# Moving four transposes behind a projection in TensorE's step of a gated recurrent block

## The chip, the cores and the metric

The kernel runs on one core of a Trainium2 chip. The time is device microseconds of one execution. The kernel before was run three times: 1324.55, 1326.75 and 1327.91 us. The engines of the core work side by side and wait for each other by semaphores: TensorE (PE), VectorE (DVE), ScalarE (ACT), GpSimd (POOL) and SyncE (SP), which issues DMAs. GpSimd issues DMAs as well.

## The reference, cut to what matters

One block over a sequence of 2048 tokens of width 512: a layer norm, an attention-like part with 16 heads of 128 over four lags, a feed-forward part with weights reduced to their signs, and their product added to the input.

```
xn = layernorm(x)                                  # 2048 x 512
q, k, v = silu(xn @ Wq), silu(xn @ Wk), silu(xn @ Wv)   # 2048 x (16*128)
z, a, b = xn @ Wz, xn @ Wa, xn @ Wb
q, k, v = causal conv of 4 taps, per channel
q, k = rotary embedding of each
q = q / max(norm(q), 1e-12); k = k / max(norm(k), 1e-12)   # per head
for s in range(4):                                 # lags
    out += (sum(q * lag(k, s)) * scale * sigmoid(lag(a, s) * b)) * lag(v, s)
out = out * rsqrt(mean(out**2) + 1e-6) * norm_w * silu(z)
s = out @ Wout
g = silu((relu((xn @ sign(up).T) * up_scale) @ sign(down).T) * down_scale * output_scale)
y = x + s * g
```

## The kernel before, in words

The attention part runs in 64 steps, 16 heads (h) times 4 chunks of 512 tokens (g); c = 4h + g is the number of the step. Every engine has its own program of 64 steps, written by hand, and each engine carries out its program strictly in the order in which it is written (`schedule`, L349). The work on one block (a head and a chunk) is spread over four steps: `back(h, g, k)` gives the block of k steps ago, named at1, at2 and at3.

PE's step (L1070) was: project q, k and v of this block, each of them 12 matmuls of 512 columns (three products of high and low parts over four tiles of the width); `turn_fold` of block c-1; project z of block c-2; `score` of block c-2; `sum_values` of block c-3. Block c-2's z takes the PSUM bank that k has just left, so PE waits for the silu of k.

The folded squares belong to the norms of q and k. ScalarE squares the rotated halves of q and k into two arrays (L703, L704), a DMA of GpSimd adds one to the other (L568), and `turn_fold` (L1047) turns the sum with four transposes of 128 columns, so that tokens lie on partitions. DVE's `sum_fold` (L839) reduces what PE has turned to norms; GpSimd makes reciprocal roots of them (L528, L532), which pass through DRAM by DMAs of SyncE and come back as part of the gates (L548 to L556) a step later.

`score` (L1057) makes a band of scores between k and q, four fp32 matmuls of 132 columns. All blocks use the same PSUM buffer for them. So PE's score of block c-2 waits until DVE has read the scores of block c-3 (`gated`, L1063). DVE reads them in `gate_scores` (L854) and masks the result in `mask_band` (L864), which `sum_values` (L1034) waits for.

DVE's step (L880) has this order: tap 1 of q; v turned; rotation of k, with taps 2 and 3 of q between; tap 1 of k; `sum_fold` of block c-1; tap 2 of k; `gate_scores` and `mask_band` of block c-3; tap 3 of k; at g = 3 the low part of the next head's weights of q; taps of v and rotation of q; `join_out` and `make_o` of block c-3; more low parts of weights.

The two lines of this that tie the engines:

```
        def sum_fold(g1, c):
            wait(dve, turned_f, c)          # PE: turn_fold of this step
        ...
        def score(g2, k):                   # in step c, k = c - 2
            wait(pe, gated, k)              # DVE: gate_scores of block c - 3, this step
```

After the 64 steps PE, DVE and the others finish the last blocks in an order of their own (L1107 to L1124), and then come the feed-forward part and the output projection.

Of the kernel before, what the change touches and what calls it, by code (L numbers as in the profile page):

```python
# [205 lines left out]
def attention(nc, env):  # L206
# [135 lines left out]
    def back(h, g, k):  # L342

        h2, g2 = (h, g - k) if g >= k else (h - 1, g - k + G)
        if isinstance(h2, int) and not 0 <= h2 < H:
            return None
        return h2, g2
# [11 lines left out]
    def is_start(h, g):  # L359
        return isinstance(h, int) and h == 0 and g == 0  # L360
# [7 lines left out]
    def cols(g):  # L368
        return slice(g * CH, (g + 1) * CH)
# [599 lines left out]
    def on_tensor(pe):  # L969
# [22 lines left out]
        def project(n, bank, h, g, c, terms=range(TERMS)):  # L992
            if terms[0] == 0:
                wait(pe, wlo_done[n], h + 1)
            for i in terms:
                w, part = ((w_hi, x_hi), (w_lo, x_hi), (w_hi, x_lo))[i // KT]
                last = nc.tensor.matmul(bank[:, :], w[n][:, i % KT, :], part[:, i % KT, cols(g)],  # L997
                                        start=(i == 0), stop=(i == TERMS - 1))
            if terms[-1] == TERMS - 1:
                last.then_inc(proj_done[n], 1)  # L1000
# [33 lines left out]
        def sum_values(g3, c):  # L1034

            wait(pe, coef_done, c - 2)
            wait_v(pe, g3, c - 3)
            wait(pe, o_done, c - 3)
            wait(pe, out_sq_done, c - 3)
            for b in range(BC):  # L1040
                at = b % 2 * P
                last = nc.tensor.matmul(two[:, b // 2, at:at + BW], v_tok[:, g3 * BC + b, :],  # L1042
                                        coef[:, g3 % 2, b, :], start=(b % 2 == 0),
                                        stop=(b % 2 == 1), skip_group_check=True)
            last.then_inc(out_done, 1)

        def turn_fold(g1, c):  # L1047
            wait(pe, norms_done, c - 1)
            if isinstance(c, int) and c == NC:
                pe.wait_ge(folded_last, 1)  # L1050
            else:
                wait(pe, folded, 16 * c)
            for b in range(BC):
                last = nc.tensor.transpose(bank_tk[:, b * P:(b + 1) * P], fold[g1 % 2][:, b * P:(b + 1) * P], ident)  # L1054
            last.then_inc(turned_f, 1)

        def score(g2, k):  # L1057
            ahead = 1 if g2 < G - 1 else 0
            wait_rope(pe, "k", g2, k)
            wait_rope(pe, "q", g2, k)  # L1060
            if ahead:
                wait_rope(pe, "q", g2 + 1, k + 1)
            wait(pe, gated, k)  # L1063
            for b in range(BC):
                at = (g2 * BC + b) * P
                last = nc.tensor.matmul(scores[:, b, :], rot["k"][:, at:at + P], rot["q"][:, at:at + BW],  # L1066
                                        start=True, stop=True)
            last.then_inc(scores_done, 1)

        def step(h, g):  # L1070
            c = h * G + g
            at1, at2, at3 = (back(h, g, k) for k in (1, 2, 3))
            if not is_start(h, g):
                wait(pe, silu_done["v"], 2 * c)
                project("q", bank_qv, h, g, c)
            if is_start(h, g - 1):
                pe.wait_ge(bx_done, LAGS + 1)
                for i in range(2):
                    own = bx[:, i * HALF_NB:(i + 1) * HALF_NB, :, :].rearrange("p b h r -> p (b h r)")
                    after = bx[:, i * HALF_NB + 1:(i + 1) * HALF_NB + 1, :, :].rearrange(  # L1080
                        "p b h r -> p (b h r)")
                    nc.tensor.matmul(pick_banks[i], sel_own, own, start=True, stop=False)
                    nc.tensor.matmul(pick_banks[i], sel_next, after, start=False, stop=True
                                     ).then_inc(picked, 1)
            if not is_start(h, g):
                wait(pe, z_done, c - 2)
                project("k", bank_kz, h, g, c)
            wait(pe, silu_done["q"], 2 * c + 2)
            project("v", bank_qv, h, g, c)
            if is_start(h, g):  # L1090
                pe.wait_ge(abt_done, G)
                for b in range(NB):
                    last = nc.tensor.transpose(bank_ab[:, b * AB:(b + 1) * AB], ab_t[:, b * P:(b + 1) * P],
                                               ident[0:AB, 0:AB])
                last.then_inc(ab_turned, 1)
            if at1:
                turn_fold(at1[1], c)
            if at2:
                wait(pe, silu_done["k"], 2 * c + 2)
                project("z", bank_kz, at2[0], at2[1], c - 2)  # L1100
            if at2:
                score(at2[1], c - 2)
            if at3:
                sum_values(at3[1], c)

        schedule(pe, step)
        wait(pe, z_done, NC - 2)  # L1107
        project("z", bank_kz, H - 1, G - 2, NC - 2)
# [497 lines left out]
```

## Time and profile before

| | |
|---|---|
| median of 3 runs | 1326.75 us |
| the profiled execution | 1327.47 us |
| its span, first to last instruction | 1325.7 us |
| mean granted clock of PE | 0.995 |
| busy: PE, DVE, ACT, POOL | 1292.8, 954.7, 720.5, 641.8 us |

A matmul's record starts when the engine takes it up and its end is modelled, so records of neighbouring matmuls overlap. Distances between starts are the safer measure. The granted clock is a share of full speed: 1.00 is 2.4 GHz and 0.50 is 1.2 GHz. The number after `x` in a timeline row is how many instructions it merges; square brackets give the idle time of the engine before the row and what ended it.

### The profile page before, as it was taken

To read this page: it belongs to the slowest core of one execution; us is meant where nothing else is said; L and a number is where in the kernel's file an instruction comes from. 1 tells how busy PE (TensorE), PEld (TensorE's weight loads), DVE (VectorE), ACT (ScalarE), POOL (GpSimd) and SP (SyncE) were. 2 spreads that over 40 slices of the span, in tenths; PEclk is the share of its full clock that TensorE was granted. 3 is DMA by queue.
4 is the path that set the end of the run, shared out by engine and by line. 5 is a ranking of instruction groups with operands and counts; after the bars stand their busy time and mean duration, and the time that the engine had idled before them with its cause. 6 is when DMAs were issued, how large, how long until landed. Compare 5 with 4: busy or idle time off the path is not lost.

```text
span 1325.7 us, 22085 instructions
## 1 busy us (share of the span) xinstructions
PE 1292.8 (98%) x6312; PEld 1078.7 (81%) x6312; DVE 954.7 (72%) x1530; ACT 720.5 (54%) x1377; POOL 641.8 (48%) x827
## 2 busy tenths in 40 slices
PE   6989999999999999999999999998999999999998
PEld 5778888888888888888888888877888888888886
DVE  7879999989999999899999998993122322423442
ACT  5656666666666666666666666664543444422221
POOL 6357676777776767767767777763000000000001
PEclk9989999999999999999999999999999999999999
DMA  8258888888797888787878787868510101246544
GB/s 267 63 108 174 157 157 157 169 149 171 139 177 149 163 155 166 153 170 142 174 153 162 150 164 154 153 121 221 178 47 18 47 16 56 85 154 213 184 124 138
DMA packets 276875, 188.89 MB, mean 142 GB/s; under 512 B 167904, under 2 KB 204768, under 8 KB 276576
## 3 DMA queue, kind: packets, MB, share of 16 engines
q1 hardware_dynamic: 238064, 121.48, 34.1%
q0 software_dynamic: 38768, 66.87, 31.1%
q8 instruction: 23, 0.38, 0.1%
q14 instruction: 20, 0.16, 0.1%
HBM read 79.36 MB, written 42.08 MB: 92 GB/s over the span
## 4 chain that ended last, share of the span: by engine, by line
PE 77%; DVE 11%; issue 5%; DMA 3%; POOL 2%; ACT 2%; SPq 1%; DVEq 0%; POOLq 0%; ACTq 0%
PE bank L997 37%; PE bank L1491 13%; PE bank L1294 9%; PE bank L1281 8%; PE bank L1066 3%; PE bank L1042 3%; DVE y_k L812 2%; DVE y_q L812 2%; PE bank L1054 2%; DVE y_v L812 2%; PE bank L987 1%; ACT y_q L676 1%; DMA rq_win<-rq_scratch 1%; DVE coef L858 1%; DVE rot_k L831 1%
## 5 line engine op out<-in xcount | busy, mean ns | idle before, releaser
L812 DVE SCALAR_TENSOR_TENSOR y_q<-u_q,cw_q,y_q 128x512 f32<-128x512 f32 x192 | 143.0, 745 | 57.7 <-ACT y_q L676 57.6
L1362 POOL TENSOR_TENSOR g_buf<-g_buf,up_raw 128x512 f32<-128x512 f32 x3 | 3.8, 1280 | 356.2 <-DVE g_buf L1422 356.2
L1270 DVE TENSOR_TENSOR hid_lo<-relu,hid_hi 128x512 fp32r<-128x512 f32 x64 | 44.3, 693 | 166.4 <-ACT hid_hi L1262 166.4
L812 DVE SCALAR_TENSOR_TENSOR y_k<-u_k,cw_k,y_k 128x512 f32<-128x512 f32 x192 | 143.4, 747 | 1.3 <-ACT y_k L676 1.1
L812 DVE SCALAR_TENSOR_TENSOR y_v<-u_v,cw_v,y_v 128x512 f32<-128x512 f32 x192 | 143.4, 747 | 0.6
L532 POOL TENSOR_TENSOR rnorm<-norms,neg_half 128x8 f32<-128x8 f32 x64 | 125.0, 1953 | 9.6 <-POOL norms L528 8.6
L574 POOL DMA_DIRECT2D rot_q<-swapped_q x128 | 107.5, 996 | 43.4 <-DVE swapped_q L835 24.1
L574 POOL DMA_DIRECT2D rot_k<-swapped_k x128 | 107.3, 977 | 38.9 <-issue 25.3
L1258 ACT ACTIVATE relu<-bank,us_sb 128x512 f32<-128x512 f32 x64 | 44.1, 690 | 126.3 <-PE bank L1281 119.2
L568 POOL DMA_DIRECT2D down_raw<-down_raw x63 | 59.2, 940 | 91.0 <-ACT down_raw L704 81.4
L1382 ACT ACTIVATE hid_hi<-o_raw 128x512 fp32r<-128x512 f32 x64 | 40.2, 630 | 115.9 <-PE bank L1491 95.2
L1442 DVE TENSOR_TENSOR hid_lo<-o_raw,hid_hi 128x512 fp32r<-128x512 f32 x64 | 43.8, 690 | 79.9 <-ACT hid_hi L1382 79.9
L1491 PE MATMUL bank<-x_hi,hid_hi 128*128 128x512 f32 x256 | 99.6, 389 | 0.0
L1491 PE MATMUL bank<-x_hi,hid_lo 128*128 128x512 f32 x256 | 99.6, 389 | 0.0
L1491 PE MATMUL bank<-x_lo,hid_hi 128*128 128x512 f32 x256 | 99.6, 389 | 0.0
L528 POOL TENSOR_SCALAR norms<-norms 128x8 f32<-128x8 f32 x64 | 97.2, 1518 | 4.9 <-DVE norms L842 4.9
L562 POOL DMA_DIRECT2D sq_sum<-out_sq x62 | 90.9, 1467 | 2.5 <-issue 2.5
L662 ACT ACTIVATE u_v<-bank 128x512 f32<-128x512 f32 x64 | 38.4, 600 | 71.0 <-PE bank L997 71.0
L1066 PEld LDWEIGHTS bank<-rot_q,rot_k 128*128 128x128 f32 x512 | 68.1, 191 | 10.3 <-issue 5.5
L997 PE MATMUL bank<-x_hi,whi_z 128*128 128x512 f32 x256 | 75.6, 417 | 0.0
L1294 PE MATMUL bank<-down_sign_b,hid_hi 128*128 128x512 f32 x192 | 74.8, 390 | 0.4 <-DVE hid_lo L1270 0.4
L1294 PE MATMUL bank<-down_sign_b,hid_lo 128*128 128x512 f32 x192 | 74.7, 389 | 0.0
(189 smaller groups left out, 3514.8 us busy)
## 6 DMA issues: line engine op xcount, KB each, us to landing
rot_q<-swapped_q POOLq DMA_DIRECT2D x128, 128.0 KB, 4.5
v_scratch<-y_v SPq DMA_DIRECT2D x64, 256.0 KB, 3.6
rot_k<-swapped_k POOLq DMA_DIRECT2D x128, 128.0 KB, 4.1
v_tok<-v_scratch SPq DMA_DIRECT2D x256, 64.0 KB, 3.8
o_scratch<-o_buf SPq DMA_DIRECT2D x64, 256.0 KB, 3.5
o_raw<-o_scratch SPq DMA_DIRECT2D x64, 256.0 KB, 4.2
down_raw<-down_raw POOLq DMA_DIRECT2D x63, 256.0 KB, 3.4
sq_sum<-out_sq POOLq DMA_DIRECT2D x62, 256.0 KB, 5.4
```

The source lines that it names most:

```text
L528: nc.gpsimd.tensor_scalar(norms[:, g1 % 2, :], norms[:, g1 % 2, :], NORM_FLOOR, None, ALU.max).then_inc(floor_done, 1)
L532: nc.gpsimd.tensor_tensor(rnorm[:, g1 % 2, :], norms[:, g1 % 2, :], neg_half[:, 0:2 * BC], ALU.pow).then_inc(root_done, 1)
L562: nc.gpsimd.dma_start(sq_sum[:, cols(g)], squares, accum_op=ALU.add).then_inc(sq_added, 16)
L568: nc.gpsimd.dma_start(fold[g1 % 2], other[g1 % 2], accum_op=ALU.add).then_inc(folded, 16)
L574: nc.gpsimd.dma_start(rot[n][to:to + HALF, cols(g1)], swapped[n][frm:frm + HALF, g1 % 2, :], accum_op=ALU.add).then_inc(rope_added[n][g1 % ...
L812: nc.vector.scalar_tensor_tensor(y[n][:, g % 2, :], u[n][:, g % 2, i:i + CH], cw[n][:, bass.ds(h * TAPS + i, 1)], y[n][:, g % 2, :], ALU.m ...
L997: last = nc.tensor.matmul(bank[:, :], w[n][:, i % KT, :], part[:, i % KT, cols(g)], start=(i == 0), stop=(i == TERMS - 1))
L1066: last = nc.tensor.matmul(scores[:, b, :], rot["k"][:, at:at + P], rot["q"][:, at:at + BW], start=True, stop=True)
L1270: nc.vector.tensor_tensor(hid_lo[:, j % HS, :], relu[:, j % 2, :], hid_hi[:, j % HS, :].bitcast(fp32), ALU.subtract).then_inc(hid_lo_done, 1)
L1281: last = nc.tensor.matmul(up_bank(n, j), up_group(j // WG)[:, t, j % WG * P:(j % WG + 1) * P], part[:, t, bass.ds(n * CH, CH)], start=(k = ...
L1294: last = nc.tensor.matmul(acc_of(n)[b], part[:, j % HS, b * P:(b + 1) * P], down_group(j // WG)[:, j % WG, :], start=(j == 0 and part is h ...
L1491: last = nc.tensor.matmul(sums[b], part[:, h % HS, b * P:(b + 1) * P], wo_tile(w, h // KT, h % KT), start=(h == 0 and k == 0), stop=(h == ...
```

## The change

In PE's step the call of `turn_fold` moves from before the projection of z to behind it. Its waits (for the fold's DMA and for DVE's earlier reduction) move with it, and the wait for the silu of k now comes first. No other engine's program is touched.

```diff
@@ -1093,11 +1093,11 @@
                     last = nc.tensor.transpose(bank_ab[:, b * AB:(b + 1) * AB], ab_t[:, b * P:(b + 1) * P],
                                                ident[0:AB, 0:AB])
                 last.then_inc(ab_turned, 1)
-            if at1:
-                turn_fold(at1[1], c)
             if at2:
                 wait(pe, silu_done["k"], 2 * c + 2)
                 project("z", bank_kz, at2[0], at2[1], c - 2)
+            if at1:
+                turn_fold(at1[1], c)
             if at2:
                 score(at2[1], c - 2)
             if at3:
```

## Rows read from the trace of the kernel before

**Rows 1.** The page, the chain that ended last, by engine.

```profile
PE 77%; DVE 11%; issue 5%; DMA 3%; POOL 2%; ACT 2%; SPq 1%; DVEq 0%; POOLq 0%; ACTq 0%
```

**Rows 2.** Busy time by stretches: stretch, its length, each engine, clock, DMA share, GB/s.

```profile
350.00:450.00 100.00, 99.48 (x514) 83.97 (x513) 94.19 (x153) 64.31 (x129) 72.39 (x92) 1.00 0.83 163
```

**Rows 3.** Timeline of PE (start, length, line, what, count, idle before), one step.

```profile
403.01 1.07 PE L997 MATMUL bank<-x_hi,whi_v 128*128 128x512 f32 x4
...
405.73 0.60 PE L1054 MATMUL bank<-const,down_raw 128*128 128x128 f32 x4
406.09 1.17 PE L997 MATMUL bank<-x_hi,whi_z 128*128 128x512 f32 x4
...
408.92 1.07 PE L1066 MATMUL bank<-rot_q,rot_k 128*128 128x132 f32 x8
409.82 1.06 PE L1042 MATMUL bank<-coef,v_tok 128*128 128x132 f32 x8
410.64 1.17 PE L997 MATMUL bank<-x_hi,whi_q 128*128 128x512 f32 x4
...
413.89 1.17 PE L997 MATMUL bank<-x_hi,whi_k 128*128 128x512 f32 x4 [0.26 <-DVE wlo_k L823]
```

**Rows 4.** Timeline of all engines, DVE's and POOL's work between the transposes and scores.

```profile
406.46 0.68 DVE L842 TENSOR_REDUCE norms<-bank 128x8 f32<-128x512 f32 x1
...
407.06 0.74 DVE L812 SCALAR_TENSOR_TENSOR y_k<-u_k,cw_k,y_k 128x512 f32<-128x512 f32 x1
...
407.71 0.70 DVE L858 TENSOR_TENSOR coef<-bank,gates 128x528 f32<-128x528 f32 x1
...
413.06 0.68 DVE L823 TENSOR_TENSOR wlo_k<-raw_k,whi_k 128x512 fp32r<-128x512 f32 x1
...
418.48 0.38 POOL L556 TENSOR_TENSOR gates<-rq_own,gate_k 128x16 f32<-128x16 f32 x1 [0.25 <-POOL rq_own L551]
...
428.82 0.75 DVE L812 SCALAR_TENSOR_TENSOR y_q<-u_q,cw_q,y_q 128x512 f32<-128x512 f32 x1 [1.23 <-ACT y_q L676]
```

**Rows 5.** Timeline of PE and DVE in steps 1 and 2.

```profile
57.25 0.60 PE L1054 MATMUL bank<-const,down_raw 128*128 128x128 f32 x4
57.88 0.69 DVE L842 TENSOR_REDUCE norms<-bank 128x8 f32<-128x512 f32 x1 [0.90 <-PE bank L1054]
...
71.32 1.08 PE L1054 MATMUL bank<-const,down_raw 128*128 128x128 f32 x4 [4.18 <-DMA down_raw<-down_raw]
...
76.99 1.07 PE L1066 MATMUL bank<-rot_q,rot_k 128*128 128x132 f32 x8
```

**Rows 6.** Timeline of PE and DVE behind the last step.

```profile
894.66 0.63 PE L1054 MATMUL bank<-const,down_raw 128*128 128x128 f32 x4 [1.19 <-DVE down_raw L934]
...
901.81 0.71 DVE L858 TENSOR_TENSOR coef<-bank,gates 128x528 f32<-128x528 f32 x1 [4.90 <-POOL gates L556]
...
902.67 2.10 PE L1066 MATMUL bank<-rot_q,rot_k 128*128 128x132 f32 x8 [2.79 <-DVE coef L858]
...
906.09 1.17 PE L1281 MATMUL bank<-x_hi,up_sign_a 128*128 128x512 f32 x4
...
911.10 1.14 PE L1066 MATMUL bank<-rot_q,rot_k 128*128 128x132 f32 x8 [1.13 <-DVE coef L858]
...
912.90 1.18 PE L1281 MATMUL bank<-x_hi,up_sign_a 128*128 128x512 f32 x4
```

**Rows 7.** Timeline of PE ahead of the first step.

```profile
38.78 1.16 PE L987 MATMUL bank<-x_hi,whi_z 128*128 128x512 f32 x4 [1.46 <-issue]
```

**Rows 8.** Busy time by stretches of half a microsecond around two long pauses of PE.

```profile
69.50:70.00 0.50, 0.00 (x0) 0.00 (x0) 0.15 (x1) 0.49 (x2) 0.50 (x2) 0.73 1.05 258
...
73.50:74.00 0.50, 0.50 (x3) 0.40 (x2) 0.47 (x2) 0.00 (x0) 0.42 (x2) 0.50 0.00 0
...
902.50:903.00 0.50, 0.33 (x1) 0.36 (x2) 0.47 (x2) 0.50 (x1) 0.42 (x1) 0.59 1.02 327
...
906.00:906.50 0.50, 0.50 (x5) 0.46 (x4) 0.00 (x0) 0.13 (x1) 0.00 (x0) 1.00 0.48 77
```

## The prediction

> **What bounds the kernel now.** I read the chain of waits first, by engine: TensorE (PE) holds 77% of it [rows 1]. The busy time by stretches comes next: in the attention stage, from 150 to 850 us, seven stretches of 100 us all look alike, with PE busy for over 99 us, VectorE (DVE) for 93 to 94, and the granted clock at 1.00, which is 2.4 GHz [rows 2]. So PE is the bound and DVE is close behind it, with under 7% of slack. That small slack makes the order in which the two engines feed each other the thing to read, and for that I used the timeline of one step.
>
> PE's step, by starts [rows 3]: the projection of v takes 405.73 - 403.01 = 2.72 us, the four transposes 0.36, z 408.92 - 406.09 = 2.83, the scores 0.90, the sums over values 0.82, q 2.83 (it too follows short matmuls). With k at 2.72, a step is 2.72 x 2 + 2.83 x 2 + 0.36 + 0.90 + 0.82 = 13.18 us. Once per head k waits for its low weights: 413.89 - 410.64 - 2.83 = 0.42 us.
>
> DVE's order in the same step [rows 4]: sum_fold (L842), which reads the transposes, then the second tap of k, then the multiply of scores by gates (L858), then the mask. The scores have one buffer: score(c-2) waits in the code for `gated`, the multiply of this same step. So the chain is transposes -> L842 -> tap -> L858 -> scores. At present the projection of z, 2.83 us, stands between its two PE ends and hides it. L858 starts at 407.71 and the scores at 408.92, with nothing late.
>
> **What the change takes away.** z now follows v, both long, so z falls from 2.83 to v's 2.72: 0.11 us, in 61 steps (c = 3 to 63) 6.7 us [rows 3]. The wait for the silu of k moves ahead of the transposes with z; that silu runs while PE is still in v, so I cost it at nothing. silu_z gets its bank 0.36 us earlier, which nobody waits for.
>
> **What it adds: a wait.** The transposes now end PE's long work, and only they let L842 start. The links are each measured. From the transposes' start to L842 where DVE was waiting for them: 57.88 - 57.25 = 0.63 us [rows 5]. L842 to the tap 407.06 - 406.46 = 0.60, tap to L858 0.65 [rows 4]. L858 to the scores where PE was waiting for it: 902.67 - 901.81 = 0.86 [rows 6]. Sum 2.74 us, of which PE fills 0.36 with issuing the transposes. PE stands still for 2.38 us between issues; in the trace's own terms, the records end 0.60 after the transposes' start, so the shown pause would be about 2.14. After a pause, scores and values take 912.90 - 911.10 = 1.80 us against 410.64 - 408.92 = 1.72 [rows 3, 6]: 0.08 more. The mask follows L858 and is over before the values want it, as in that row.
>
> Steps that pay are those with an L858 in them and a turn_fold: c = 3 to 63, 61 of them. Net 2.38 - 0.11 + 0.08 = 2.35 us, x 61 = 143.4 us. The bounds of the stall are 0 (if L858 weren't behind L842 in DVE's order, which the code excludes) and 2.74 (if the transposes' issue hid nothing).
>
> Does the lateness grow on the other queues? DVE: everything behind L842 is late with it. In a normal step DVE now waits 1.23 us for q's tap (428.82) [rows 4]; the step grows by 2.35 us and DVE's work by nothing, so it stands at L842 ahead of the transposes and isn't a second bound. GpSimd: floor and power hang on L842's norms, SyncE's exchange of 1/|q| hangs on them, and the gates end 418.86 - 406.46 = 12.4 us after the reduction of the step before [rows 4]. The multiply that wants them comes a period plus 1.25 us after that reduction, at least 15.5 + 1.25. They are in time. The swapped halves and the folded squares start from work behind L858 or from q's taps and get more time before the scores and transposes that want them.
>
> The weights once per head: k's low half starts 413.06 - 407.71 = 5.35 us after L858 and k's projection 6.18 after it [rows 3, 4]. PE reaches k 0.86 + 1.80 + 2.83 = 5.49 after L858, so k would wait 0.69 rather than 0.42: 15 x 0.27 = 4.1 us. If scores and values run slower (below) PE arrives later than 6.18 and even the old 15 x 0.42 = 6.3 us go.
>
> **The start.** In step 2 PE idles 4.18 us until a fold's DMA lands, and only then does z, at half clock; scores start at 76.99 [rows 5]. With the change z runs in that pause. The next limit is the swapped q, whose DMAs are over at 73.5, as the DMA share falls to 0.00 there [rows 8]. So 76.99 - 73.5 = 3.5 us are gained once. Bounds: 0, and 5.3 (scores 0.36 behind the transposes of 71.32).
>
> **The clock.** Two long pauses of PE in this trace cost it its clock: after 4.18 us (0.73 in the half microsecond from 69.50) and after 2.79 us (0.59 from 902.50, back at 1.00 from 906.00) [rows 5, 6, 8]. Pauses of 1.13, 1.19 and 1.46 us did not [rows 6, 7]. The new one, 2.14 in the same terms, lies midway. But the 2.79 us had full-length matmuls on its front side, and the new pause has short ones on both sides, transposes ahead and 1.80 us of scores and values behind, so PE does less around it. And it comes back every step. I take it that the clock is lost in most steps. The price of one loss: scores and values took 906.09 - 902.67 = 3.42 us at 1.2 GHz against 1.80 at 2.4, so 1.62 us [rows 6]. Bounds over the stage: 0 and 61 x 1.62 = 98.8. I take 56 of 61 losses, 90.7 us.
>
> The Trainium skill, "TensorE: Matmul & The Clock Gate", section "Why this matters for your kernels", warns only of idle gaps longer than the one worked out here. By that rule the clock stays at 2.4 GHz and rival A below is the outcome. The trace has no pause of this size to decide it; its 2.79 us is shorter than the page's limit and did lose the clock, so I lean against the rule.
>
> **Sum**, against the profiled execution (1327.47 us, its span 1325.7): 1327.5 + 143.4 (wait, net) - 3.5 (start) + 90.7 (clock) - 6.3 (k's wait covered) = 1551.8. The profiled execution is 0.7 above the median, so against the median I say 1551.
>
> **The rivals.**
> A. The clock holds. Same wait, no loss: 1327.5 + 143.4 - 3.5 + 4.1 = 1471.5, about 1471. For it: 1.46 us was harmless. Against: 2.79 wasn't.
> B. The clock falls in some steps only, a third to two thirds: 20 to 40 losses, 32 to 65 us, with k's wait partly kept: 1500 to 1535. It would need the same pause to lose the clock at one time and keep it at another.
> C. Faster: the short matmuls stand together at no wait. One mechanism: PE reaches the scores no earlier than L858 + 0.86, because L842 is off DVE's road to L858. Then only the 0.11 us x 61 and the start count: 1327.5 - 6.7 - 3.5 = 1317. It decides where transposes to L858 take less than the transposes themselves, 0.36 us; the links measured sum to 1.88 to L858's start. Only a misreading of DVE's order would bring it.
> D. The change does not do what it says: short matmuls together save nothing, since scores and values need the same time behind transposes as behind z. That moves the sum by under 7 us and isn't told apart by the time.
>
> **How the numbers follow.** Forecast (clock lost nearly everywhere, 1535 to 1565) 0.60; B 0.17; A 0.18; C 0.02; beyond 1570, by something late that I've not seen, 0.03. The range must reach A to hold 8 in 10 with some room: 1466 to 1568. The likeliest case's own range is 1535 to 1565. About 0.3% (4 us) is what can be told from no change here. Faster 0.02, same 0.01, slower 0.97.
>
> **What would show it.** Order on PE: v, z, then L1054, L1066, L1042. Before L1066 a pause of some 2.1 us released by L858, in 61 steps. Before L842 on DVE a wait for L1054 in each. z's twelve matmuls 2.72 us. A step of 15.5 us where the clock is 1.00 and some 17.1 where it fell. PE's busy share down to some 86% of a step, and the granted clock below 1.00 in the attention slices, near 0.9. What follows the last scores unchanged, 1325.7 - 911.1 = 415 us. The prediction is wrong if L1066 isn't released by L858, if the pause is under 1.5 us, or if the clock stays at 1.00 throughout (then A).

## The result: 1551.2 us, and the profile after

The changed kernel takes 1551.16 us (1550.53 to 1554.31, 4 runs) against 1327.33 us for the kernel before on the same chip. The ratio is 1.1691, 95% interval 1.1675 to 1.1707: 17% slower.

The page of the changed kernel, in four rows: the busy time of the engines, the granted clock in 40 slices, the chain that ended last by engine, and the costliest group with the idle time ahead of it.

```profile
PE 1390.5 (90%) x6312; PEld 1165.4 (75%) x6312; DVE 962.0 (62%) x1530; ACT 717.9 (46%) x1377; POOL 612.7 (40%) x827
PEclk9999899989998998899999989988999999999999
PE 87%; DVE 7%; issue 4%; DMA 1%; POOL 1%; ACT 0%; SPq 0%; DVEq 0%; POOLq 0%
L1066 PE MATMUL bank<-rot_q,rot_k 128*128 128x132 f32 x512 | 99.2, 353 | 137.3 <-DVE coef L858 136.6
```

The scores (L1066) did not head any list before. Now PE idles 136.6 us for L858 just ahead of them. In the second row each digit is one of 40 slices, and a 9 stands for 90% or more; the eight digits of 8, all within the attention stage, are slices whose mean clock was under 0.9. That PE's share of the chain rose from 77% [rows 1] to 87% is no sign of more work: it is the same 6312 matmuls, some of them at half clock.

One stretch of 700 us inside that stage, first of the kernel before and then of the changed one (busy time of PE's matmuls, its weight loads, DVE, ACT and POOL, then clock, DMA share and GB/s, as in [rows 2]):

```profile
150.00:850.00 700.00, 696.72 (x3580) 588.32 (x3579) 653.00 (x1053) 444.57 (x893) 505.05 (x634) 1.00 0.83 159
```

```profile
150.00:850.00 700.00, 610.48 (x2792) 517.75 (x2791) 514.70 (x823) 346.36 (x699) 375.27 (x492) 0.91 0.63 124
```

PE is busy 87% instead of 99.5%, at a clock of 0.91. DVE falls from 93% to 74%, so it did not become the bound.

PE's timeline over one step of the changed kernel, to be laid beside [rows 3]:

```profile
474.70 1.07 PE L997 MATMUL bank<-x_lo,whi_v 128*128 128x512 f32 x4
475.61 1.07 PE L997 MATMUL bank<-x_hi,whi_z 128*128 128x512 f32 x4
...
478.33 0.60 PE L1054 MATMUL bank<-const,down_raw 128*128 128x128 f32 x4
481.08 1.96 PE L1066 MATMUL bank<-rot_q,rot_k 128*128 128x132 f32 x8 [2.15 <-DVE coef L858]
482.83 1.96 PE L1042 MATMUL bank<-coef,v_tok 128*128 128x132 f32 x8
484.44 1.27 PE L997 MATMUL bank<-x_hi,whi_q 128*128 128x512 f32 x4
...
495.55 0.60 PE L1054 MATMUL bank<-const,down_raw 128*128 128x128 f32 x4
```

z takes 478.33 - 475.61 = 2.72 us. Scores stand 2.75 us behind the transposes, with a recorded pause of 2.15. The two short groups take 484.44 - 481.08 = 3.36 us where they took 1.72. The step is 495.55 - 478.33 = 17.22 us long.

DVE and GpSimd in the same step, with the chain that makes the pause [rows 4]:

```profile
478.96 0.69 DVE L842 TENSOR_REDUCE norms<-bank 128x8 f32<-128x512 f32 x1 [2.59 <-PE bank L1054]
479.57 0.74 DVE L812 SCALAR_TENSOR_TENSOR y_k<-u_k,cw_k,y_k 128x512 f32<-128x512 f32 x1
...
480.23 0.70 DVE L858 TENSOR_TENSOR coef<-bank,gates 128x528 f32<-128x528 f32 x1
...
490.28 0.23 POOL L556 TENSOR_TENSOR gates<-rq_own,gate_k 128x16 f32<-128x16 f32 x1
```

The links are 0.63, 0.61, 0.66 and 0.85 us. The 2.59 us in brackets is DVE standing at the reduction; the tap and the multiply behind it then start with no wait of their own, so what they need was ready. The order of one engine's work, not its load, sets the end.

The clock around the same pause (half microseconds of the changed kernel):

```profile
480.50:481.00 0.50, 0.00 (x0) 0.00 (x0) 0.47 (x2) 0.00 (x0) 0.42 (x1) 1.00 0.01 0
481.00:481.50 0.50, 0.42 (x2) 0.45 (x3) 0.50 (x1) 0.00 (x0) 0.50 (x1) 0.73 0.00 0
481.50:482.00 0.50, 0.50 (x4) 0.50 (x4) 0.50 (x2) 0.00 (x0) 0.50 (x1) 0.50 0.00 0
...
484.50:485.00 0.50, 0.50 (x4) 0.46 (x3) 0.00 (x0) 0.18 (x1) 0.00 (x0) 0.86 0.00 0
485.00:485.50 0.50, 0.50 (x4) 0.41 (x3) 0.47 (x2) 0.48 (x2) 0.00 (x0) 1.00 0.00 0
```

PE is at 2.4 GHz while it stands still and falls to 1.2 GHz just as it has resumed. The half speed lies from about 481.23 to 484.64, 3.41 us, here on top of work. The mean granted clock of the whole span is 0.937, so (1 - 0.937) / 0.5 x 1549.1 = 195 us ran at 1.2 GHz, as much as 57 stretches of this length. The clock's own record in the trace has 56 of them, one in 56 of the 61 steps from 3 to 63, and a last one that reaches into the end of the span.

So five steps kept the clock, and their pause was no shorter. One of them, and the next to last scores of the stage, with the clock of three stretches:

```profile
532.67 1.14 PE L1066 MATMUL bank<-rot_q,rot_k 128*128 128x132 f32 x8 [2.15 <-DVE coef L858]
...
1127.48 1.14 PE L1066 MATMUL bank<-rot_q,rot_k 128*128 128x132 f32 x8 [2.81 <-DVE coef L858]
```

```profile
532.00:548.00 16.00, 13.41 (x68) 11.23 (x68) 13.01 (x21) 8.45 (x17) 9.74 (x14) 1.00 0.66 129
548.00:565.00 17.00, 15.01 (x68) 12.59 (x68) 11.70 (x20) 8.85 (x18) 9.00 (x13) 0.90 0.62 112
1126.00:1131.00 5.00, 3.52 (x24) 3.27 (x25) 1.66 (x3) 1.38 (x3) 1.36 (x3) 1.00 1.02 206
```

A step without the loss takes 548.23 - 532.67 = 15.56 us from scores to scores, and one with it 17.20 (the median, outside the steps that wait for k's weights): one loss costs 1.64 us. The pause of 2.81 us, behind long matmuls, did not cost the clock, where the one of 2.79 at the same place of the kernel before did [rows 6, 8]. Over the ten profiles of this case the pause at this place is 2.79 to 2.83 us; seven lost the clock around it and three kept it (this kernel and, below, the reduction between mask and tap 3 and the late reduction with PE's old order). The length of the pause alone does not decide. In the trace the half speed also begins at another place of each step: 1.27 us behind the start of the scores at 548.23, then a little earlier from step to step, until it begins 0.19 ahead of them at 720.35; the step after that one keeps the clock. What sets this place was not tested.

The 223.4 us between the two spans (1549.1 and 1325.7) are divided below, from scores to scores. Rows of the changed kernel, step 2 and the end, beside [rows 5, 6]:

```profile
57.77 0.60 PE L1054 MATMUL bank<-const,down_raw 128*128 128x128 f32 x4
...
71.69 0.63 PE L1054 MATMUL bank<-const,down_raw 128*128 128x128 f32 x4 [1.31 <-DMA down_raw<-down_raw]
73.01 1.14 PE L1066 MATMUL bank<-rot_q,rot_k 128*128 128x132 f32 x8 [0.69 <-DMA rot_q<-swapped_q]
...
87.67 1.14 PE L1066 MATMUL bank<-rot_q,rot_k 128*128 128x132 f32 x8 [2.15 <-DVE coef L858]
...
1134.52 1.14 PE L1066 MATMUL bank<-rot_q,rot_k 128*128 128x132 f32 x8 [1.36 <-DVE coef L858]
```

| stretch | before | after | difference |
|---|---|---|---|
| up to the transposes of step 1 | 57.25 | 57.77 | +0.5 |
| to the scores of step 2 | 19.74 | 15.24 | -4.5 |
| to the last scores | 834.11 | 1061.51 | +227.4 |
| from there to the end | 414.60 | 414.58 | 0.0 |

### The profile page after: what moved, and what is told of

The parts are those of the page before. It is cut to its first block, busy times and chain, and to the rows that moved or that the text cites. A ratio compares the mean times of both kernels' runs of the same rounds, so it can differ in the third digit from the quotient of the medians.

```text
span 1549.1 us, 22085 instructions
## 1 busy us (share of the span) xinstructions
PE 1390.5 (90%) x6312; PEld 1165.4 (75%) x6312; DVE 962.0 (62%) x1530; ACT 717.9 (46%) x1377; POOL 612.7 (40%) x827
## 4 chain that ended last, share of the span: by engine, by line
PE 87%; DVE 7%; issue 4%; DMA 1%; POOL 1%; ACT 0%; SPq 0%; DVEq 0%; POOLq 0%
PE bank L997 45%; PE bank L1491 11%; PE bank L1294 7%; PE bank L1281 7%; PE bank L1042 6%; PE bank L1066 6%; DVE y_k L812 3%; DVE coef L858 3%; PE bank L1054 2%; PE bank L987 1%; PE bank L974 0%; DMA rot_q<-swapped_q 0%; DVE norms L842 0%; DMA up_raw<-in_x 0%; PE bank L1013 0%
## 5 line engine op out<-in xcount | busy, mean ns | idle before, releaser
L1066 PE MATMUL bank<-rot_q,rot_k 128*128 128x132 f32 x512 | 99.2, 353 | 137.3 <-DVE coef L858 136.6
L1066 PEld LDWEIGHTS bank<-rot_q,rot_k 128*128 128x128 f32 x512 | 83.6, 244 | 151.0 <-issue 151.0
L688 ACT ACTIVATE carry<-bank 128x8 f32<-128x8 f32 x64 | 11.3, 177 | 312.8 <-PE bank L1042 312.8
L842 DVE TENSOR_REDUCE norms<-bank 128x8 f32<-128x512 f32 x64 | 44.4, 693 | 157.6 <-PE bank L1054 157.6
L574 POOL DMA_DIRECT2D rot_q<-swapped_q x128 | 114.5, 1105 | 23.0 <-DVE swapped_q L835 18.8
L1042 PE MATMUL bank<-coef,v_tok 128*128 128x132 f32 x512 | 114.5, 398 | 0.4 <-ACT swapped_q L696 0.4
L532 POOL TENSOR_TENSOR rnorm<-norms,neg_half 128x8 f32<-128x8 f32 x64 | 107.8, 1685 | 9.7 <-POOL norms L528 8.7
L1042 PEld LDWEIGHTS bank<-coef,v_tok 128*128 128x128 f32 x512 | 108.5, 307 | 0.8 <-issue 0.8
L997 PE MATMUL bank<-x_hi,whi_q 128*128 128x512 f32 x252 | 98.4, 524 | 0.5 <-ACT u_v L671 0.5
```

What stands on the lines that cost most here:

```text
L532: nc.gpsimd.tensor_tensor(rnorm[:, g1 % 2, :], norms[:, g1 % 2, :], neg_half[:, 0:2 * BC], ALU.pow).then_inc(root_done, 1)
L574: nc.gpsimd.dma_start(rot[n][to:to + HALF, cols(g1)], swapped[n][frm:frm + HALF, g1 % 2, :], accum_op=ALU.add).then_inc(rope_added[n][g1 % ...
L842: nc.vector.tensor_reduce(norms[:, g1 % 2, :].rearrange("p (n b) -> p b n", b=BC), bank_tk[:, :].rearrange("p (b n d) -> p b n d", b=BC, n=2),
```

## The experiments

**The reduction behind tap 3 of k.**

```diff
             conv_tap("k", 1, h, g, c)
-            if at1:
-                sum_fold(at1[1], c)
             conv_tap("k", 2, h, g, c)
             ...
             conv_tap("k", 3, h, g, c)
+            if at1:
+                sum_fold(at1[1], c)
```

> The changed kernel with DVE's sum_fold moved from behind tap 1 of k to behind tap 3 of k, so that gate_scores and mask_band stand ahead of it. Theory (the wait runs over DVE's order, and the pause costs the clock): no pause before the scores, clock 1.00, so 1327 - 4.4 (start, as the changed kernel's trace shows) - 61 x 0.11 (z behind v) = 1316; if the norms, now 2.6 us later, make GpSimd's gates late, up to 0.5 us a step more, 1346. Rival 1 (transposes, scores and values in a row are slow on PE by themselves): DVE's order changes nothing, about 1551. Rival 2 (the wait is as I say, but the clock falls because short matmuls stand together, not because PE pauses): 1316 plus 56 losses of 1.6 us, about 1406.

It took 1345.53 us, ratio 1.0141 (1.0121 to 1.0160), with PE's mean clock at 0.996. PE's program is the one of the changed kernel, and 206 us are gone by two lines on DVE. So the short matmuls side by side are not slow, and without the pause they do not cost the clock; both rivals fall. The 20 us that stay over the kernel before are the late gates that the expectation named, with 1346 as its upper end. DVE, GpSimd and SyncE in this kernel:

```profile
444.76 0.69 DVE L842 TENSOR_REDUCE norms<-bank 128x8 f32<-128x512 f32 x1
...
450.17 0.58 SPq L412 DMA_DIRECT2D rq_win<-rq_scratch  x1
...
455.74 0.24 POOL L548 TENSOR_TENSOR rq_win<-rq_win,const 128x32 f32<-128x32 f32 x1 [4.03 <-DMA rq_win<-rq_scratch]
456.05 0.22 POOL L551 TENSOR_TENSOR rq_own<-rq_win 128x16 f32<-128x16 f32 x1
...
456.35 0.23 POOL L556 TENSOR_TENSOR gates<-rq_own,gate_k 128x16 f32<-128x16 f32 x1
...
456.71 0.71 DVE L858 TENSOR_TENSOR coef<-bank,gates 128x528 f32<-128x528 f32 x1 [1.45 <-POOL gates L556]
...
458.74 0.69 DVE L842 TENSOR_REDUCE norms<-bank 128x8 f32<-128x512 f32 x1
```

From the reduction at 444.76 through roots, exchange and gates back to the multiply is 11.95 us, and 2.03 more to the next reduction: 13.98 us for a round, above a step of 13.2. The multiply waited for the gates 39 times, 44.3 us in all, of which part was slack. A late reduction thus has its own price, by another road: GpSimd and the exchange through DRAM.

**The late reduction alone, with PE's old order.** The same edit of DVE on the kernel before.

> The kernel before on PE (transposes ahead of z), with DVE's sum_fold behind tap 3 of k. It tells the price of the late reduction by itself. Theory (the round over the gates sets the step): the reduction stands at the same place of DVE's order as in the run that took 1345.5, so 1345 to 1352. Rival (PE's new order made those 20 us): 1327.

1347.74 us, ratio 1.0148 (1.0130 to 1.0167); the multiply waits 44.0 us for the gates, as above. PE's order makes no difference to these 20 us. The rival falls.

**The reduction between mask and tap 3.** One link earlier than in the first run.

```diff
                 mask_band(at3[1], c - 3)
+            if at1:
+                sum_fold(at1[1], c)
             conv_tap("k", 3, h, g, c)
```

> The changed kernel with DVE's sum_fold between mask_band and tap 3 of k. Theory: with the reduction behind tap 3 the kernel took 1345.5 us because the round norms - roots - exchange - gates - gate_scores - reduction closes in 11.9 + 2.0 = 14.0 us against a step of 13.2; here the reduction follows gate_scores by 1.4 us and not 2.0, so the round takes 13.3: 1345.5 - 0.65 x 40 = 1320, at best 1316. Rival (the 20 us over 1326 come from the order of PE, not from the gates): 1345 again.

1330.15 us, ratio 1.0032 (1.0018 to 1.0046). The direction from 1345.5 is right, and the size was a miss of 10 us; no gain over the kernel before is left, the whole interval lies above 1. The gates no longer hold the multiply (9.7 us in 6 waits), so the round was cured as expected. What I had wrong is the gain that I thought lay behind it. PE's timeline of a step in which it waits for nothing:

```profile
456.90 1.07 PE L997 MATMUL bank<-x_hi,whi_z 128*128 128x512 f32 x4
...
459.62 0.60 PE L1054 MATMUL bank<-const,down_raw 128*128 128x128 f32 x4
460.05 1.07 PE L1066 MATMUL bank<-rot_q,rot_k 128*128 128x132 f32 x8
460.96 1.06 PE L1042 MATMUL bank<-coef,v_tok 128*128 128x132 f32 x8
```

z is 2.72 us, as foreseen, but the transposes in front of the scores take 0.43 and not 0.36. Of the 0.11 us per step 0.04 is left: 2.4 us over the stage, not 6.7. And DVE is now held at the reduction (22.0 us in 52 waits between 150 and 850 us), which delays the low halves of the weights: PE waits 5.6 us for k's and 3.7 for q's, where it waited 3.9 for k's alone. Between starts of scores such a step takes about 14.32 us (the one from 460.05 to 474.39 is an example) against 13.72 before, some 9 us in 15 heads. So putting the short matmuls together is worth next to nothing here even when no wait comes with it.

**The reduction behind tap 2.** The chain from transposes to scores loses one tap.

```diff
-            if at1:
-                sum_fold(at1[1], c)
             conv_tap("k", 2, h, g, c)
+            if at1:
+                sum_fold(at1[1], c)
```

> The changed kernel with DVE's sum_fold behind tap 2 of k, just ahead of gate_scores: one link of 0.65 us less between transposes and scores. Theory: the wait falls by 0.65 us in 61 steps, 40 us, and the pause from 2.15 to 1.50 us. If 1.50 us keeps the clock, as the 1.46 us did in the kernel before: 1551 - 40 - 91 + 10 = 1430. If the clock falls still: 1511. Rival (PE's matmuls in a row are slow by themselves): 1551.

1431.80 us, ratio 1.0795 (1.0775 to 1.0814), clock 0.998: 119 us less for 0.65 us of work moved out of the chain. A row of it:

```profile
450.09 1.15 PE L1066 MATMUL bank<-rot_q,rot_k 128*128 128x132 f32 x8 [1.49 <-DVE coef L858]
```

By 61 x 0.65, 40 us of the 119 are the shorter wait. The rest, 79 us, I put down to the clock, which this pause doesn't lose.

**The pause filled.** Nine matmuls of 512 columns between transposes and scores, from step 3 on, into a bank that nothing reads in these steps. They add work and leave the result alone.

```diff
             if at1:
                 turn_fold(at1[1], c)
+            if at3:
+                for _ in range(9):
+                    nc.tensor.matmul(banks[2][:, :], x_hi[:, 0, 0:P], x_hi[:, 0, cols(0)],
+                                     start=True, stop=True)
             if at2:
                 score(at2[1], c - 2)
```

> The changed kernel with nine matmuls of 512 columns between the transposes and the scores, from step 3 on, written to a bank that nothing reads. They take 9 x 0.227 = 2.04 us of the 2.39 us in which PE waits. Theory (the pause costs the clock): the wait is the same, the pause shrinks to some 0.3 us, the clock stays at 1.00: 1551 - 56 x 1.62 + 15 x 0.69 = about 1471. Rival (the clock falls for the short matmuls beside each other): clock near 0.93 and about 1551 still. If PE's own chain were the limit and not DVE, the nine would add 61 x 2.04 = 124 us: 1675.

1471.95 us, ratio 1.1102 (1.1084 to 1.1121), clock 0.997. Nine matmuls more per step, 549 in all, make the kernel 79 us faster. A pass of it:

```profile
448.56 0.60 PE L1054 MATMUL bank<-const,down_raw 128*128 128x128 f32 x4
448.91 2.31 PE L1103 MATMUL bank<-x_hi 128*128 128x512 f32 x9
451.31 1.14 PE L1066 MATMUL bank<-rot_q,rot_k 128*128 128x132 f32 x8
```

Scores start 2.75 us behind the transposes, exactly as without them: the wait is DVE's and the filling hides in it. This separates the two parts of the loss: the wait costs 1471.95 - 1326 = 146 us (after the gain at the start), the clock 79, after what the waits for k's weights give back.

**One and two matmuls in the pause.** The same edit with `range(2)` and `range(1)`; one such matmul is called a filler below.

> The changed kernel with two idle-time matmuls between transposes and scores, where nine kept the clock. The wait for DVE is the same, the pause is 2.15 - 2 x 0.23 = 1.7 us. If the clock holds, 1472; if it falls in all steps, 1551; between them if it falls in some. My guess, since 1.5 us kept it: mostly kept, 1480.

1470.41 us, ratio 1.1078 (1.1059 to 1.1097), clock 0.998, pause 1.70 us.

> As the run with two, with one matmul: pause 1.9 us. Kept 1472, lost 1551. My guess is that it lies between, some 1520, since this pause is just under the one of the changed kernel that lost the clock in nearly every step.

1542.50 us, ratio 1.1631 (1.1598 to 1.1665), pause 1.92 us. Its four executions spread more than those of the other kernels, from 1533.68 to 1547.88 us, with mean clocks from 0.951 to 0.938; the profiled one is the fastest, with 0.951. Its row and that of the run with two:

```profile
451.75 1.25 PE L1066 MATMUL bank<-rot_q,rot_k 128*128 128x132 f32 x8 [1.92 <-DVE coef L858]
```

```profile
448.76 1.14 PE L1066 MATMUL bank<-rot_q,rot_k 128*128 128x132 f32 x8 [1.70 <-DVE coef L858]
```

Two such fillers keep the clock in every step from 3 to 63. With one it is lost in many steps and kept in others at the same pause: (1 - 0.951) / 0.5 x 1531.9 = 150 us at half speed, as much as 44 stretches of 3.41 us, and in the trace 42 of the 61 steps have one. The slowest execution, at 0.938, is nearly at the changed kernel's 0.937. I had guessed 1520 for the one; the step between the two is steeper than that. A second filler of 0.23 us is worth 72 us. A filler both shortens the pause and adds work ahead of the scores; the run with the reduction behind tap 2 only shortens it. Which of the two saves the clock with fillers isn't shown.

**The new order in step 2 alone.** All other steps as before.

```diff
+            second = isinstance(c, int) and c == 2
-            if at1:
+            if at1 and not second:
                 turn_fold(at1[1], c)
             if at2:
                 wait(pe, silu_done["k"], 2 * c + 2)
                 project("z", bank_kz, at2[0], at2[1], c - 2)
+            if second:
+                turn_fold(at1[1], c)
```

> The kernel before, with the transposes behind z in step 2 alone; all other steps keep the old order. Theory (the gain at the start is real and lasts): 1327.3 - 4.4 = 1323, and the clock stretch near 70 us gone. Rival (given back by a later wait of the first steps, the gates of step 3 or the weights): 1327.

1323.12 us against 1325.84, ratio 0.9982 (0.9971 to 0.9992): 1.1 to 3.8 us faster. It is the one version that beats both kernels. Its trace has the whole effect at the place (transposes of step 1 to scores of step 2):

```profile
56.93 0.60 PE L1054 MATMUL bank<-const,down_raw 128*128 128x128 f32 x4
...
70.45 0.63 PE L1054 MATMUL bank<-const,down_raw 128*128 128x128 f32 x4 [0.92 <-DMA down_raw<-down_raw]
71.89 1.14 PE L1066 MATMUL bank<-rot_q,rot_k 128*128 128x132 f32 x8 [0.82 <-DMA rot_q<-swapped_q]
```

That is 14.96 us against 19.74. The timed gain is smaller than these 4.8 us. The execution of the kernel before that was profiled is itself 1.6 us above its median, and it ran z at half speed at this place; whether its other executions did isn't shown, and the rest stays open.

## Why the prediction was right, point by point

*The chain.* Its four links were 0.63, 0.60, 0.65 and 0.86 us and were measured at 0.63, 0.61, 0.66 and 0.85: 2.75 against 2.74. The first and the last had been taken from places of the old trace where the second engine was really waiting for the first [rows 5, 6], the two between from DVE's own succession [rows 4], and all four held. The recorded pause was to be 2.14 and is 2.15. The reduction moved by one place in DVE's order (1431.8 us) and behind the multiply (1345.5 us) shows that it is this chain.

*No growth on other queues.* DVE stood waiting at the reduction (2.59 us), gates and halves were in time, as forecast. The wait for k's weights went from 3.9 us to 0.4, as forecast for steps at half clock.

*The clock.* This was the open choice, 0.60 for nearly every step. 56 losses of 61 were assumed at 1.62 us each, and the trace has 56 at 1.64: 92 us against 90.7. That the loss would come in most steps was judged between pauses on either side; that the count of 56 is met exactly is luck, since nothing in the rows gave it. The stated range reached down to rival A's 1471, so the range alone would not have told the two apart. The reason given, that a pause with short matmuls on both sides leaves PE less to do, was not tested by itself. The pair that the choice leaned on is weaker evidence than it looked: 2.79 us lost the clock before, and a pause of that length at the same place kept it in three of the ten profiles. In the other long pause of the old trace the clock fell at about 69.73, some 2.6 us into the 4.18 and not at their end. Rival B wanted the same pause to lose the clock at one time and keep it at another; this happens, in 5 of 61 steps here and in 19 of 61 with one filler, only too seldom here to bring B's time.

The run with two fillers, which waits alike and keeps the clock, is 1551.2 - 1470.4 = 80.8 us faster. To this come k's waits, which are back there: 5.3 us more in PE's own idle time, some 12 by the distances between starts (16.43 us for such a step against 15.56, where the changed kernel has about 17.28 against 17.20). That makes 86 to 93 us for the clock, in line with the count. Rival A's sum, 1471, is what the filled kernels took, 1470.4 and 1472.0. Its reason, that the clock holds in a pause of this length, is refuted for all but those five steps. The Trainium skill's rule of "TensorE: Matmul & The Clock Gate", section "Why this matters for your kernels", asks only to avoid longer gaps; here pauses of 2.15 and 1.92 us lost the clock in most steps, and the measurement decides.

*The start.* -4.5 us against -3.5: the DMAs of the swapped q were over by the 73.01 of the scores rather than the 73.5 that I read from the DMA share, and from the transposes of step 1 to those of step 2 it took 13.92 us rather than 14.07.

*A saving that needs the pause.* In the changed kernel z did become 0.11 us shorter in each step, and a step that keeps the clock is 15.56 - 13.18 = 2.38 us longer against the 2.35 of the sum. But up to the scores the transposes take 0.43 us behind z where they took 0.36 up to z. Here the pause swallows this; where there is none, only 0.04 of the 0.11 remain. It made rival C's 1317 and the expectation of 1320 too low.

*The sum.* From the scores of step 2 on, 143.4 + 90.7 - 6.3 = 227.8 met 227.4. Small errors cancel in it: the waits for k's weights cost 0.53 us per head before by starts (13.71 against 13.18), not 0.42, and one loss of the clock that the kernel before had behind the last step, 1.62 us, is gone from the changed one.

## What to carry to other kernels

Before work is moved on the bounding engine, look at what the other engine has in its order between the two ends of the moved piece: work of 2.8 us that stood between cause and effect was the cover of a 2.7 us chain, and taking it away cost 2.4 us in each of 61 steps. A short wait on TensorE can have a second price beside its own length: here a pause of 2.15 us cost 1.64 us more by the clock in 56 of 61 steps, and either 0.45 us of idle matmuls or one link less in the chain gave that back. The version that came out ahead, by 1.1 to 3.8 us, makes the move only in step 2, where PE waited for a DMA anyhow. Moving matmuls of one kind together is by itself worth some hundredths of a microsecond per step.

## What the runs showed of the hardware

The clock was kept with recorded pauses of 1.49 (1431.8 us) and 1.70 us (1470.4 us) in every step from 3 to 63. It was lost in 42 of these 61 steps with 1.92 (the execution of 1533.7 us) and in 56 with 2.15 (1550.9 us). All these pauses stand ahead of the same short matmuls, behind transposes or, in the filled kernels, a long matmul. Steps that lost it and steps that kept it have the same pause, and pauses of 2.79 to 2.83 us behind the last step lost it in seven profiles and kept it in three, so no length read here is a bound that holds by itself. The loss read above lasted 3.41 us at 1.2 GHz and fell on the short matmuls and the head of q's projection. Two matmuls that compute nothing, 0.45 us of PE's time per step, are enough to keep it.
